# One of a chunk's eight normalised columns moves from VectorE to GpSimd

## The reference, cut to what matters

```
x = x + conv(ln_c(x))        # conv: depthwise 3x3 with taps, 'SAME', and y + its own input
t = tokens(x)
t = t + ffn(ln_t(t))         # ffn: 96 -> 384 -> 96, float8 multiplies, float16 sums, relu
```

## Time and profile before

| what | value |
|---|---|
| time, median of 3 runs | 3422.01 us (3416.06 to 3424.34) |
| the profiled execution: its time, its span | 3413.97 us, 3412.2 us |
| TensorE busy | 3017.2 us, 88% |
| VectorE busy | 3207.9 us, 94% |
| ScalarE busy | 3155.9 us, 92% |
| GpSimd busy | 1921.0 us, 56% |
| DMA | 714.47 MB, mean 209 GB/s |

### The profile page before, as it was taken

The page is one execution under the profiler, slowest core; times in us unless marked ns, Lnnn a source line. Parts: engine busy times, 40 slices in busy tenths (PEclk is TensorE's granted clock), DMA queues, the critical chain, the costliest instruction groups (busy, mean ns, idle before and its releaser), DMA issues.

```text
span 3412.2 us, 87581 instructions
## 1 busy us (share of the span) xinstructions
PE 3017.2 (88%) x24902; PEld 2505.6 (73%) x24902; DVE 3207.9 (94%) x11739; ACT 3155.9 (92%) x7100; POOL 1921.0 (56%) x915
## 2 busy tenths in 40 slices
PE   3299999999999899989999999989999999999976
PEld 3287777777777777777777777777777777778744
DVE  5447999999999999999999999999999999999998
ACT  5578999999999999999999999999999999987776
POOL 0003666656666566656666566665666666666676
PEclk9999999999999999999999999999999999999966
DMA  4567777777777777777777777777777777766533
GB/s 146 160 195 210 229 227 222 223 213 225 223 228 222 205 224 227 224 207 231 222 225 224 213 224 227 224 219 219 222 221 229 226 222 223 228 200 183 162 119 101
DMA packets 277335, 714.47 MB, mean 209 GB/s; under 512 B 34809, under 2 KB 34914, under 8 KB 276834
## 3 DMA queue, kind: packets, MB, share of 16 engines
q1 hardware_dynamic: 271394, 694.12, 69.5%
q10 hardware_dynamic: 5440, 14.45, 1.3%
HBM read 539.84 MB, written 168.59 MB: 208 GB/s over the span
## 4 chain that ended last, share of the span: by engine, by line
DVE 62%; issue 14%; ACT 10%; PE 8%; DMA 4%; DVEq 1%; SPq 0%; ACTq 0%; POOL 0%; POOLq 0%
DVE stats L602 21%; DVE xq L639 18%; DVE hid L592 9%; PE conv_ps L387 5%; ACT images L476 5%; DVE images L652 4%; DVE hid L597 4%; ACT hid L455 3%; DMA xn<-in_x 2%; DVE xt_ps L626 2%; PE hid_ps L350 1%; DVE rstd L630 1%; DMA band_ring<-bands 1%; DVE neg_mean L634 1%; PE y_ps L365 1%
## 5 line engine op out<-in xcount | busy, mean ns | idle before, releaser
L387 PE MATMUL conv_ps<-images,band_ring 112*112 112x222 f32 (+1 forms) x9216 | 1941.0, 356 | 49.5 <-DMA band_ring<-bands 48.9
L387 PEld LDWEIGHTS conv_ps<-images,band_ring 112*112 112x112 f32 x9216 | 1605.6, 178 | 205.5 <-issue 47.2
L236 POOL TENSOR_TENSOR xf<-xf,y 112x768 f32<-112x768 f32 x448 | 951.8, 2124 | 1169.0 <-DVE y L619 1169.0
L455 ACT ACTIVATE hid<-hid_ps 128x896 f16<-128x896 f32 x1344 | 1190.7, 926 | 90.1 <-PE hid_ps L350 87.4
L231 POOL TENSOR_TENSOR xf<-xf,images 112x768 f32<-112x768 f32 x448 | 981.3, 2190 | 318.2 <-DMA xf<-in_x 302.8
L476 ACT ACTIVATE images<-xn,neg_mean,rstd 112x96 f32<-112x96 f32 x2688 | 1082.2, 555 | 28.8 <-DVE neg_mean L634 19.3
L365 PEld LDWEIGHTS y_ps<-w2t,hid 128*128 128x128 f16 x10752 | 575.7, 100 | 408.5 <-ACT hid L455 217.2
L365 PE MATMUL y_ps<-w2t,hid 128*128 128x96 f16 x10752 | 672.3, 210 | 207.5 <-ACT hid L455 182.5
L639 DVE SCALAR_TENSOR_TENSOR xq<-xf,stats,xt_ps 112x96 fp8e5<-112x96 f32 x3584 | 850.1, 332 | 0.0
L350 PE MATMUL hid_ps<-xt,w1t 96*128 96x448 fp8e5 x2688 | 683.1, 363 | 23.6 <-ACT xt L447 23.6
L592 DVE TENSOR_SCALAR hid<-hid,b1q 128x896 f16<-128x896 f16 x1344 | 609.3, 489 | 16.0 <-ACT hid L455 14.9
(11 more groups left out here) (51 smaller groups left out, 692.8 us busy)
## 6 DMA issues: line engine op xcount, KB each, us to landing
band_ring<-bands SPq DMA_DIRECT2D x768, 294.0 KB, 5.1
xn<-in_x SPq DMA_DIRECT2D x448, 336.0 KB, 3.4
xf<-in_x SPq DMA_DIRECT2D x448, 336.0 KB, 5.0
out<-xf SPq DMA_DIRECT2D x448, 336.0 KB, 3.8
bands<-images ACTq DMA_DIRECT2D x4, 3528.0 KB, 15.1
xf<-in_L_ffn_W SPq DMA_DIRECT2D x2, 144.0 KB, 2.9
xf<-in_L_conv_kernel SPq DMA_DIRECT2D x3, 3.4 KB
xf<-in_L_ffn_b SPq DMA_DIRECT2D x1, 42.0 KB, 3.0
```

Source lines behind the costliest of these rows:

```text
L236: pool.tensor_tensor(res, res, y[:, e % 2], ALU.add).then_inc(summed, CW)
L387: mm = pe.matmul(dst[:, :, lo:hi], band_ring[:, n % BAND_RING, PAIR * dx + i, :], images[:, m % 2, :, ch, lo + dx - 1:hi + dx - 1], start= ...
L455: nc.scalar.activation(hid[:, e % 2, TOK * j:TOK * (j + 1)].rearrange("p (u n) -> p u n", u=2), hid_ps[:, k, :, 0:HALF * H], ACT.Identity) ...
```

## The change

GpSimd gets a `normalise` of its own for column 7, VectorE keeps column 6 (`DVE_COLS = 1`), ScalarE keeps its six. GpSimd signals a third semaphore, `normed_pool`, which enters the list `normed`, so everything that waited for that list waits for GpSimd too. GpSimd's column is issued last in its step, behind `add_ffn` and `add_conv`; two waits stand ahead of `add_conv`.

```
-        normed = [sem("normed_act"), sem("normed_dve")]
+        normed = [sem("normed_act"), sem("normed_dve"), sem("normed_pool")]
...
+                def normalise(r, n):
+                    b, i, cols = chunk_at(n)
+                    if n < LOOP:
+                        pool.wait_ge(rstd_c_done, n + 1)
+                    if n == STAGED_FROM:
+                        for s in bands_out:
+                            pool.wait_ge(s, 16)
+                    for w in range(ACT_COLS + DVE_COLS, CW):
+                        op = pool.tensor_scalar(images[:, b, i, :, cols.start + w], xn[:, n % NORM_RING, w, :],
+                                                stats[:, n % 2, 1, w, 1:2], rstd[:, n % 2, w:w + 1],
+                                                ALU.subtract, ALU.mult)
+                    op.then_inc(normed[2], 1)
+
                 def step(r, c, t):
 
                     if ffn_in(t - 3):
                         add_ffn(r, c - 3)
+                    if norm_in(t + 1) and c + 1 >= 0:
+
+                        wait(pool, rstd_c_done, LOOP * r + c + 2 + LOOP)
+                        wait(pool, with_conv, LOOP * r + c + 2)
                     if ffn_in(t + 2):
                         add_conv(r, c + 2)
+                    if norm_in(t + 1):
+                        normalise(r, c + 1 + LOOP)
...
-                    for w in range(ACT_COLS, CW):
+                    for w in range(ACT_COLS, ACT_COLS + DVE_COLS):
                         op = dve.tensor_scalar(images[:, b, i, :, cols.start + w], xn[:, n % NORM_RING, w, :],
```

More of the change, by code:

```diff
@@ L26 @@
 ACT_COLS = 6
+DVE_COLS = 1
 EPS_C = 1e-6
```

## The result

The changed kernel takes 4645.76 us, median of 4 runs (4641.0 to 4660.61), against 3419.74 us for the kernel before on the same chip: ratio 1.3592, 95% interval 1.3556 to 1.3627. The forecast was slower, at 4260 us with a range of 3990 to 4520; the sign and the mechanism came out, the size lies outside the range.

A forecast was written before the change was run, and what follows sets the result against it. VectorE and ScalarE were taken to set the pace at 6.92 us a step. After the change, a ring of 8.96 plus 0.15 for collisions, 9.11 us over 388 steps, adds 843 us: 4260, range 3990 to 4520.

The forecast's parts named there:

- The ring: Loop of waits, one turn per step: column's end, `xn` issue, `xf` issue, landing, `add_conv`, column; sum 8.96 us.
- hand-over to SyncE: Time from the end of GpSimd's column to SyncE's issue of the `xn` load, put at 0.16 us.
- `xn` to `xf` issue: Time in SyncE's queue between issuing these two loads, with the store between, put at 1.11 us.
- landing and start: `xf` load from issue to landing, 5.0 us (ends 4.5 and 6.1), then 0.10 until `add_conv` starts.
- the column at 0.40: GpSimd's new 96-element instruction, taken as 0.40 us; ends 0.18 and 1.63, most of the weight below 0.7.
- its collisions at 0.15: GpSimd meeting VectorE: a held-up L592 could slip in ahead of the column, adding 0 to 0.45 us a step, taken 0.15.
- the two waits ahead of `add_conv`: GpSimd's waits for `rstd_c_done` and `with_conv`, claimed to be already met when reached, cost 0.
- The phases: Times after the column's end: `add_conv` runs from 6.4 to 8.6 us, VectorE reaches L592 at about 6.5.
- The estimate of 4380 us: Time if the shared-port rule makes the full 0.45 us due whenever L592 stands waiting: a step of 9.4 us.
- (a): Rival: the slack absorbs the late `xf` load, so not slower; time 3300 to 3422; chance 0.05.
- (b): Rival: landing at 4.5, column at 0.26, no collisions, 8.3 us a step, time 3950; chance of under 4000: 0.12.
- (c): Rival: TensorE falls to the low clock in each step, a step of 10.0 us and time 4610; chance 0.13.

## Why the prediction was right in its mechanism and wrong in size

**The ring stands.** Every part of it was found where it was put: SyncE's `load_xn` waits for GpSimd, `add_conv` for `xf`, in 353 steps. Taking the column from behind `add_conv` gives back all but 44 us, and taking `xf` from behind the column's wait, with `xn` right behind it, all but 142; leaving the column out and keeping the wait does not.

**Term by term.** Forecast against the turn measured above: hand-over to SyncE 0.16 against 0.23; `xn` to `xf` issue 1.11 against 1.07; landing and start 5.10 against 4.95; `add_conv` 2.19 against 2.17. Together 8.56 against 8.42. The error is in the last two terms, the column at 0.40 and its collisions at 0.15: 0.55 against a mean of 1.47 us. These 0.92 us x 388 are 357 of the 386 us by which the forecast fell short. With 1.47 in the forecast's sum the step is 10.03 us; from 290.99 to 4288.22 us the starts of `add_conv` lie 10.12 us apart in the mean, loop boundaries included, 10.02 in the median. The turn shown is on the short side in one term: `xf` issue to the start of `add_conv` takes 5.21 in the mean over all steps, against its 4.95 and the forecast's 5.10. Of the two waits ahead of `add_conv`, both put at 0, the one for VectorE's reciprocal held it 18 times, 74 us in all.

**The step that failed** is the one that priced the column. Its length alone was mis-sized: 0.40 was taken from selects over other data, and the instruction took 0.77 undisturbed. I had an upper end that covered it, 1.63, and then put "most of the weight below 0.7". And its collisions were bounded by 0 and 0.45, from one VectorE instruction slipping ahead. The measured cost was 0.7 in the mean (1.47 - 0.77), above the upper end. VectorE's side of such a meeting:

```profile
2013.15 2.26 DVE L612 TENSOR_SCALAR hid<-hid,b1q 128x896 f16<-128x896 f16 x1
2015.33 0.15 DVE L654 SCALAR_TENSOR_TENSOR neg_mean<-stats,rstd 112x8 f32<-112x8 f32 x1
2015.41 0.40 DVE L672 TENSOR_SCALAR images<-xn,stats,rstd 112x96 f32<-112x96 f32 x1
2015.68 0.81 DVE L612 TENSOR_SCALAR hid<-hid,b1q 128x896 f16<-128x896 f16 x2
```

The first L612 is held until `add_conv` ends at 2015.17 and ends 0.24 us later; the column, started at 2015.14, ends at 2016.69, 0.2 us after the other two L612 (2016.49). So it was not one instruction that got ahead but, by these ends, three; the run with the thin bias additions bears this out for the last two. The phases were forecast to 0.7 us: after the column's end at 2016.69, `add_conv` starts at 6.25 (6.4 forecast) and the next L612, at 2023.87, at 7.2 (6.5). What was missed is that the ring fixes VectorE's L612 group just behind `add_conv` in nearly each step, so the worst case is the usual one. The range took the unknown column to about 1 us and had no case with both ends high.

The Trainium skill, page "SBUF — State Buffer", section "Who interferes with whom", says that the one that issues first holds the shared pair for its whole instruction and the other is blocked. The lengthened L612, 2.26 us against 0.45, agrees, though it ended only 0.24 us after `add_conv` and not its whole 0.45. The column does not follow from that sentence alone: it started 0.54 us before the other two L612 (2015.14 and 2015.68) and still ended after them. The estimate of 4380 us that I drew from it was too low, since it took one instruction ahead of the column and the short column.

**The rivals.** (a), the slack holds, did not come: it needed a landing under 3.0 us, and it was 4.9. (b), a shorter ring, neither. (c), TensorE at its low clock, came in part and did not decide, though its 4610 us lie nearest to the measurement: the granted clock is 0.88 in the mean against 0.99, and 0.50, that is 1.2 GHz, from 1582 to 1586 us for one, but the ring has no TensorE in it, and its terms alone give 9.97 us in the turn above. Only in 25 of 388 steps did `add_conv` wait for VectorE or ScalarE instead of its load. How much of the last 0.1 us is the clock's wasn't separated.

**Not tried:** a deeper `xn` ring, by which SyncE would wait for an older chunk's column; TensorE's part at a fixed clock.

## What to carry to other kernels

Before giving an idle engine a small piece of work, look for who waits for the end of it and what stands behind that waiter in its queue: here a load of two slots' depth put every other transfer behind GpSimd's last instruction, and the same piece at the head of GpSimd's step was free. When a queue entry is moved, check the entries it is moved behind: `load_xn` at the end of SyncE's step closed another ring, and behind `load_xf` it left VectorE waiting 44 to 116 us for `xn`. Price an instruction that no row shows by its upper end too, and when a ring fixes the phases of two engines, take a collision between them as due in each step.

## What the runs showed of the hardware

- A GpSimd tensor_scalar over 112 x 96 float32 elements took 0.77 us with none of VectorE's float16 bias additions beside it (median, column between the additions), where an addition of 768 elements took 1.63 to 2.19: the small instruction costs far more than its share of elements. A one-element addition took 0.22 us at the head of the step and 0.34 behind `add_conv`, in the median.
- Beside VectorE's float16 bias additions the same instruction took 1.54 us; with two of the three cut to two elements, 0.91. At the head of GpSimd's step it took 2.00 in the mean.
- An `xf` load took 4.9 us in the median at 154 GB/s of traffic, and 5.0 at 222 GB/s, each time with a load and a store issued just ahead of it: the emptier queue did not shorten it. With `load_xn` moved behind it in the kernel before it took 4.4 (400 to 3000 us).
